# Causal attention with sixteen-wide heads: V's products in two column halves, each between two score products

## What is computed

```python
x = x + attn(layernorm(x))
qkv = lora_linear(hidden_states, w_attn, b_attn, la_attn, lb_attn)
q, k, v = to_heads(q), to_heads(k), to_heads(v)   # 2 x 16 heads x 1024 x 16
k, v = fake_quant(k, kv_scale, kv_zero_point), fake_quant(v, kv_scale, kv_zero_point)
scores = jnp.einsum('bhqd,bhkd->bhqk', q, k) / math.sqrt(HEAD_DIM)
scores = jnp.where(causal, scores, -jnp.inf)
attn = jax.nn.softmax(scores, axis=-1)
out = jnp.einsum('bhqk,bhkd->bhqd', attn, v)
```

## Time and profile before

| | us |
|---|---|
| median of 3 runs | 2869.5 |
| lowest and highest | 2867.05, 2874.61 |
| the profiled execution | 2889.04 |
| its span, first to last instruction | 2887.4 |
| the stage that is changed, from its first score to its last product of outputs | about 318 of the span, 106 to 424 |

### The profile page before, as it was taken

How to read it: one execution, slowest core, us unless ns; L and a number is a source line. 1 busy time by engine, 2 the same in 40 slices (tenths; PEclk the granted TensorE clock), 3 DMA queues, 4 the chain that set the end, 5 groups by cost and what they waited for, 6 DMA issues and landing times. The chain is left out here.

```text
span 2887.4 us, 37973 instructions
## 1 busy us (share of the span) xinstructions
PE 2051.4 (71%) x13661; PEld 1045.7 (36%) x13661; DVE 1699.3 (59%) x3151; ACT 994.9 (34%) x1732; POOL 934.1 (32%) x1098
## 2 busy tenths in 40 slices
PE   7698878775689871999998824444839593348992
PEld 4233335224322350222222412331414273247991
DVE  4766635674378642788886157996683505445442
ACT  3467752330034330677667202110110211134330
POOL 2122211350234404576553111232361101342325
PEclk9789978897889985899999656555869796579996
DMA  5100000000100014001100220000101100342113
GB/s 178 42 23 21 21 13 19 1 2 13 21 1 1 6 45 174 23 27 30 34 27 8 85 81 8 2 2 15 60 29 40 35 0 5 109 161 85 52 45 98
DMA packets 82081, 118.57 MB, mean 41 GB/s; under 512 B 18981, under 2 KB 58929, under 8 KB 80881
## 3 DMA queue, kind: packets, MB, share of 16 engines
q1 hardware_dynamic: 73313, 104.29, 11.2%
q0 software_dynamic: 3664, 9.32, 1.1%
q10 hardware_dynamic: 4928, 2.62, 0.3%
HBM read 78.65 MB, written 37.29 MB: 40 GB/s over the span
## 5 line engine op out<-in xcount | busy, mean ns | idle before, releaser
L1234 DVE TENSOR_REDUCE a_mx<-a_SM 128x2 f32<-128x1024 f32 x256 | 300.6, 1217 | 66.6 <-PE a_SM L1116 66.6
L1217 ACT ACTIVATE a_P<-a_ST 128x512 f32<-128x512 f32 x512 | 280.5, 594 | 120.1 <-PE a_ST L1142 120.0
L924 ACT ACTIVATE a_P<-a_ST,a_scale 128x512 f32<-128x512 f32 (+3 forms) x384 | 206.3, 588 | 84.1 <-PE a_ST L836 82.5
L939 DVE TENSOR_REDUCE a_mx<-a_SM 128x2 f32<-128x1024 f32 (+1 forms) x192 | 176.2, 951 | 66.8 <-PE a_SM L801 37.8
L1142 PE MATMUL a_ST<-a_Q,a_K 98*128 98x512 bf16 (+1 forms) x512 | 178.9, 397 | 16.4 <-ACT a_P L1217 7.4
L771 POOL TENSOR_SCALAR_AFFINE_SELECT a_P<-a_P 128x128 f32<-128x128 f32 (+1 forms) x256 | 77.1, 306 | 242.7 <-ACT a_P L924 241.5
L1156 PE MATMUL a_OP<-a_P,a_V 128*32 128x512 f32 x1024 | 140.4, 622 | 0.0
L3106 POOL CAST work<-work 128x512 bf16<-128x512 f32 x92 | 73.5, 838 | 202.9 <-PE experts_py L3190 188.5
L3256 DVE TENSOR_TENSOR experts_hl<-work 128x512 bf16<-128x512 f32 x92 | 83.8, 969 | 89.6 <-POOL work L3106 89.6
L836 PE MATMUL a_ST<-a_Q,a_K 50*128 50x512 bf16 (+3 forms) x384 | 119.3, 358 | 24.1 <-ACT a_P L924 23.7
L1116 PE MATMUL a_SM<-a_K,a_Q 48*128 48x512 bf16 x512 | 83.7, 403 | 64.2 <-DMA a_K<-k_stacks 58.1
(11 more groups left out here) (548 smaller groups left out, 4874.4 us busy)
## 6 DMA issues: line engine op xcount, KB each, us to landing
work<-L_ffn_W SPq DMA_DIRECT2D x16, 1024.0 KB, 6.2
conv_tab<-dft_tables SPq DMA_DIRECT2D x8, 1024.0 KB, 4.7
bias_hankel<-bias_rows SPq DMA_DIRECT2D x16, 448.0 KB, 3.5
expert_rows<-zeros SPq DMA_DIRECT2D x1, 5888.0 KB, 23.1
experts_xs<-expert_rows SPq DMA_DIRECT2D x23, 256.0 KB, 2.9
expert_results<-params SPq DMA_DIRECT2D x23, 256.0 KB, 2.2
a_K<-k_parts SPq DMA_DIRECT2D x32, 96.0 KB
a_Q<-q_parts SPq DMA_DIRECT2D x32, 96.0 KB
```

What stands on the lines that cost most here:

```text
L924: act.activation(Pr[:, s % 2, u, j, c0:N], ST[:, u, c0:N], ACT.Exp, scale=kscale[:, 0:1]).then_inc(exp_done, 1)
L939: dve.tensor_reduce(mx[:, g % 2, qt, k0 // N, :], SM[:, c % 2, :, 0:kn], AX.X, ALU.max).then_inc(mx_read, 1)
L1217: act.activation(Pr[:, s % 2, u, j, :], ST[:, (4 * s + x) % 2, :], ACT.Exp, scale=scale).then_inc(exp_done, 1)
L1234: dve.tensor_reduce(mx[:, g % 2, qt, k0 // N, :], SM[:, c % 2, :, :], AX.X, ALU.max).then_inc(mx_read, 1)
```

## The change

Values gets a second argument, the part. Part 0 stands behind score 1 of the next step and takes the columns 0 to 255 of the 512; part 1 stands where all of it stood, behind score 2, and takes the columns 256 to 511. Where OP is started anew (a is 0, steps 0 and 2) part 0 takes all 512 columns and part 1 nothing. Products whose visible columns all lie in one half are left out of the other: the blocks of steps 1 and 5 are seen only by columns from 256 and from 384 on, so their part 0 has no product. All waits for probabilities stand in part 0, and stay there where it has no product.

```diff
--- before.py
+++ after.py
@@ -837,23 +837,28 @@
                                      Qs[r, g % slots, qh * N + c0:(qh + 1) * N], start=True, stop=True)
                     last.then_inc(st_ready, 1)
 
-                def values(s):
+                def values(s, part):
                     g, n = divmod(s, ns)
                     qh, a = steps[n]
+                    if part == 1 and a == 0:
+                        return
                     if n == 0:
                         pe.wait_ge(v_ready, 2 * g + 2)
                     if a == 0 and 2 * g + qh:
                         pe.wait_ge(ot_done, 2 * g + qh)
-                    if n in diagonals:
+                    if part == 0 and n in diagonals:
                         pe.wait_ge(cleared, 4 * (g * len(diagonals) + diagonals.index(n) + 1))
-                    else:
+                    elif part == 0:
                         pe.wait_ge(exp_done, 4 * s + 4)
+                    end = N // 2 if part == 0 and a else N
                     for u in range(2):
                         for j in range(2):
-                            r, c0 = 32 * (2 * u + j), visible(qh, a + j)
-                            last = pe.matmul(OP[r:r + 32, c0:N], Vs[:, g % 2, u, a + j, :], Pr[:, s % 2, u, j, c0:N],
-                                             start=a == 0, stop=n == last_of[qh], skip_group_check=True)
-                    last.then_inc(pv_done, 1)
+                            r, c0 = 32 * (2 * u + j), max(visible(qh, a + j), part * N // 2)
+                            if c0 < end:
+                                last = pe.matmul(OP[r:r + 32, c0:end], Vs[:, g % 2, u, a + j, :], Pr[:, s % 2, u, j, c0:end],
+                                                 start=a == 0, stop=n == last_of[qh], skip_group_check=True)
+                    if end == N:
+                        last.then_inc(pv_done, 1)
 
                 def outputs(g, half):
                     pe.wait_ge(ot_done, 2 * g + half + 1)
@@ -884,15 +889,18 @@
                     if event(rows_at, s):
                         rows(*event(rows_at, s))
                     scores(s, 1)
+                    if s:
+                        values(s - 1, 0)
                     maxima(cut[0], cut[1])
                     scores(s, 2)
                     if s:
-                        values(s - 1)
+                        values(s - 1, 1)
                     if event(outputs_at, s):
                         outputs(*event(outputs_at, s))
                     scores(s, 3)
                     maxima(cut[1], hi)
-                values(NG * ns - 1)
+                for part in range(2):
+                    values(NG * ns - 1, part)
                 outputs(NG - 1, 1)
 
             @block.scalar
```

## The result

| | before | after |
|---|---|---|
| median, us | 2869.9 (4 runs) | 2921.82 (4 runs) |
| lowest and highest | 2867.05, 2874.61 | 2912.73, 3009.5 |
| the profiled execution | 2889.04 | 2912.73 |
| a pair at the full clock, copy of step 1 to copy of step 1 | 18.71 | 20.52 |
| the stage, first chunk to last product of outputs | 333.6 (90.2 to 423.8) | 373.1 (89.8 to 462.9) |

The changed kernel is slower: after over before is 1.0169, with a 95% interval from 1.0126 to 1.0211. The median rose by 52 us; 2934 was forecast.

A forecast was written before the change was run, and what follows sets the result against it. A loop of waits between PE and ACT, neither full, was taken to set the pace; 2869.5 + 33.4 (2.09 a pair, 16 pairs) + 31.1 (low clock) = 2934 us, range 2890 to 2995.

The forecast's parts named there:

- Rival (a): Waits cost what was forecast, clock falls no more often than before: 2903 us; chance 0.30.
- (b): Clock low nearly throughout the stage, 12 more low pairs, 93.2 us: 2996 us; chance 0.12.
- (d): Change does less than it says, slack in step 3 and gain in step 4 cancel the rest: 2870 us; chance 0.06.
- (c): Faster, less ACT idling before exponential 3, if OP's copy is done when score 1 is issued: 2847 us; chance 0.06.
- step 1: V's products stay gated by the copy; chunk and score 2 move behind them, outputs and score 3 0.41 us later.
- step 3: V's products stay gated by the copy; chunk and score 2 come behind them, exponential 3 starts 0.97 us later.
- step 4: V's products in two halves: 0.15 us for the split, 0.10 for the second entry into full-height products, 0.25 in all.
- step 5: Split and second entry as in step 4, plus 0.07 us for the earlier wait for clearing: 0.32 in all.
- steps 0, 2: Only the earlier wait for clearing: 0.14 us in step 0, or nothing if a short chunk makes it up; nothing in step 2.
- Four more pairs: Clock term: longer PE idle times put four more pairs at 1.2 GHz, 7.77 us each, 31.1 us.

The follow-up runs named there:

- wait_only: Kernel before with only PE's wait for the copy of OP moved from V's products to behind score 1, no product moved or split; 2935.19 us, 1.0191.
- move_only: Kernel before with only the whole products of steps 0 and 2 moved behind score 1 of the next step, none split; 2935.18 us, 1.0177.
- copy_first: Changed kernel with ACT's copy of OP moved ahead of exponential 0 in steps 1 and 3; 2916.02 us, 1.0114 to the kernel before.
- split_in_place: Kernel before with both halves of V's products back to back where the whole stood, behind score 2; 2874.9 us, 0.9978.
- wait_filled: wait_only with five throwaway products ahead of the moved wait in steps 1 and 3; 2887.55 us, 1.0025 to the kernel before.
- after_filled: Changed kernel with five throwaway products ahead of the wait for the copy of OP in steps 1 and 3; 2906.6 us, 1.0081 to the kernel before.

## Why the prediction was right

**The mechanism.** It was the one forecast: the start of V's products in steps 1 and 3 is set by ACT's copy, so moving them only puts chunk and score 2 behind that wait. wait_only shows it without any product moved: the wait alone makes the pair 0.88 longer, the products behind it make it 1.20 (move_only), and the halves add 0.62. The sign, the range and the two kinds of cost (pair and clock) held. Rival (a) is out: the low end of the interval is 2906, above its 2903 (2899 with the pairs as measured). (b) is out for the profiled execution, where eleven of the fifteen distances from copy to copy are 20.52 or 20.53, but its 2996 is near the three executions of 3009.5 to 3025.01, and for those it is open. (d), no change, is out by the interval. (c) failed at the point it was said to hang on, and copy_first shows that reaching it is not enough.

**The terms of the pair.** Positions are counted from the copy of step 1 (249.21 before, 203.84 after).

| | forecast | measured | read from |
|---|---|---|---|
| step 1 | 0.41 | 0.33 | score 3 at +2.69, now 206.86, +3.02 |
| step 3 | 0.97 | 0.85 | score 1 of step 4 at +9.76, now 214.78, +10.94; less 0.33 |
| step 4 | 0.25 | 0.22 | score 1 to score 3: 2.84, now 217.84 - 214.78 = 3.06 |
| step 5 | 0.32 | 0.36 | score 1 to score 3: 1.46 (0.47 to the products, 0.99 for them), now 220.73 - 218.91 = 1.82 |
| steps 0, 2 | 0.14 | 0.05 | what is left of 1.81 |
| sum | 2.09 | 1.81 | |

16 x 1.81 is 29.0 us where 33.4 was forecast.

**Terms that were mis-sized.** In step 3 the chunk behind the products takes 0.28 (212.76 to 213.04), not the 0.39 read from score 1 to score 2 in before; the 0.44 of step 0 was made from it. That is nearly the whole of the miss in step 3. The reading failed because a wait ended that distance, not the chunk. Score 2 waits for exponential 0, as the description of the kernel says, and this is ACT in before, with exponential 0 of step 1 last in the first row and that of step 3 last in the second:

```profile
248.27 1.05 ACT L924 ACTIVATE a_P<-a_ST,a_scale 128x512 f32<-128x512 f32 x2 [0.19 <-PE a_ST L836]
...
254.43 1.84 ACT L924 ACTIVATE a_P<-a_ST,a_scale 128x512 f32<-128x512 f32 x3
```

They end at 249.32 and 256.27, and score 2 starts 0.06 after each (249.38, 256.33), as V's products start 0.05 after the end of the copy (256.75, 256.80). In step 1 the chunk takes 0.18 (226.04 to 226.22) where I had 0.26, by the same misreading, and the score 0.15 (to 226.37) as forecast: 0.33. The gap in step 3 was 0.86 by issue as forecast: score 1 at 210.69, 0.21 of columns, products at 211.76; the row prints 0.68, since it counts from the end of the 0.39 with its latency.

**A step that failed in its reason.** For steps 4 and 5 I took 0.15 as the price of the split itself, from two groups of 0.57 against one of 1.00. split_in_place shows that the split costs nothing. With c for 256 columns of all four blocks and e for the visit, c + e is 0.57 (also where all four have 256, 215.10 to 215.67) and 2c + e is 1.00, so c is 0.43 and e 0.14: it is paid once for every visit of PE to V's products, however many instructions they are; whether on coming or on leaving, the rows don't say. Halves that lie apart pay it twice, so the sum still came out near the measured one. The page cited in the prediction, the Trainium skill's "TensorEngine Tiling (Array Packing)", Key Properties, fits these runs: halves back to back, with no change of tiling between them, cost nothing, and halves with a chunk and a score between them cost 0.22 (step 4) and, with the earlier wait, 0.36 (step 5).

**The clock.** Four more pairs, 31.1 us, stood for something that no row could tell: the four was chosen between bounds, and that it came near is in part luck. Read from the ratio, the change costs 48.5 us, of which 29.0 are the pairs, so some 20 are left for the clock. Filling the two gaps gives back 25 (0.0088 between two ratios that are each known to 0.003, so some 13 to 38 us). Both terms of the forecast were too large, 33.4 for 29.0 and 31.1 for 20 to 25. In the profiled execution the stage has 36.0 us more at the low clock, some 12 us, and it is the fastest execution; the slower ones have a lower mean clock. The kind was right, the place only in part. In wait_only the falls follow gaps of two thirds of a microsecond, two in every pair, and filling them ends the falls (wait_filled: 190.8 to 43.1 us at the low clock). But in the two profiled executions of after most of what is added at the low clock is a longer stretch at the stage's start, of which the prediction says nothing, and which after_filled has too. The rule cited from the Trainium skill, "TensorE: Matmul & The Clock Gate", A second HAM failure mode, that brief and frequent idling makes the clock swing, is borne out by wait_only and wait_filled. What these runs don't settle is why that first stretch ends at 114.4 in before, at about 136 in after, and at 164.8 in copy_first and after_filled, and why wait_only and move_only, with shorter pairs than after and the same gaps, spend almost twice as long at the low clock.

## What to carry to other kernels

Before a product is moved up in a list worked off in order, ask what its start hangs on: if it is a wait that ends late, what stood ahead of it was free cover, and it now stands behind. A wait is part of the move, and can be tried without the move. Where PE stands still in every turn of a loop, if only for two thirds of a microsecond, look at the granted clock as well as at the turn: in after the clock cost 20 to 25 us beside 29 for the pairs, in the profiled execution of wait_only some 39 beside 14. And a distance between two starts is the length of what lies between them only if the second start did not wait for something else.

## What the runs showed of the hardware

- With two idle times of 0.6 and 0.7 us on PE in each pair of 19.6 us (wait_only) the clock was at 1.2 GHz in 191 of the stage's 385 us. Filled with products of no use, at the same pair length (wait_filled), it was 43 of 340 us, and 48 us came off the kernel.
- In before, whose wait of 0.29 us is shorter, two throwaway products lengthen the pair by 0.15 us, and yet the kernel is no slower (0.9975, 0.9956 to 0.9994), its mean clock is higher (0.823 or more in nine of ten executions, 0.822 at most in before beside it), and its profiled execution has no fall in mid-stage.
- The four float products of a step, each with an output of 32 rows and 512 columns, take 1.00 us together, whether as 8 instructions (256.80 to 257.80) or as 16 (193.37 to 194.37 in split_in_place).
- A us at the low clock makes this loop 0.32 us longer (7.77 us for 23.9 at the low clock). PE's idle time takes up a part of what its longer products cost: it is busy 16.46 of 18.70 us at the full clock and 23.65 of 24.00 at the low one.
